# The self-attention block's feed-forward products, each taken from three products of rounded parts and rests

## The reference, cut to what matters

```python
y = y @ Wo + x
z = _rms_norm(y, ln2_w)
z = jax.nn.relu(z @ W1) @ W2      # W1 256x1024, W2 1024x256
return z + y
```

## Time and profile before

| | |
|---|---|
| median of 3 runs | 1431.43 us (1429.8 to 1434.38) |
| the profiled execution | 1430.63 us, of which 1428.8 us are its span |
| mean granted TensorE clock | 0.961 of full |
| PE busy | 1275.9 us, 89% |
| PE weight loads | 929.8 us, 65% |
| DVE busy | 766.8 us, 54% |
| ACT busy | 583.0 us, 41% |
| POOL busy | 390.7 us, 27% |

### The profile page before, as it was taken

One profiled execution on the slowest core, in us unless ns is written; L12 is line 12 of the kernel. 1 busy time (PEld: TensorE's weight loads), 2 busy tenths in 40 slices (PEclk: granted clock), 3 DMA queues, 4 the chain that ended last, 5 costly groups with the idle time before them and its releaser, 6 DMA issues.

```text
span 1428.8 us, 27261 instructions
## 1 busy us (share of the span) xinstructions
PE 1275.9 (89%) x8838; PEld 929.8 (65%) x8839; DVE 766.8 (54%) x2053; ACT 583.0 (41%) x1253; POOL 390.7 (27%) x680
## 2 busy tenths in 40 slices
PE   6588999999999999999999999999987449999997
PEld 4365776767777776767777777767765325555554
DVE  5645566676766666676666666676643241121111
ACT  3424436363545536363544536363522212222221
POOL 2311121212141221213141221213122124444443
PEclk9598999999999999999999999999999669999999
DMA  8300000000000000000000000000054002112111
GB/s 273 97 8 9 16 1 31 1 29 0 29 29 0 29 0 29 0 29 0 29 29 0 29 0 29 0 29 22 2 192 177 30 22 62 53 56 60 59 55 38
DMA packets 44135, 56.69 MB, mean 40 GB/s; under 512 B 6486, under 2 KB 38016, under 8 KB 44097
## 3 DMA queue, kind: packets, MB, share of 16 engines
q1 hardware_dynamic: 37824, 41.23, 8.8%
q0 software_dynamic: 5616, 14.43, 3.5%
q10 hardware_dynamic: 656, 0.52, 0.1%
HBM read 40.44 MB, written 16.65 MB: 40 GB/s over the span
## 4 chain that ended last, share of the span: by engine, by line
PE 75%; DVE 10%; ACT 8%; issue 5%; POOL 1%; DMA 0%; ACTq 0%; DVEq 0%; SPq 0%; POOLq 0%
PE bank L1337 69%; PE bank L1372 2%; ACT a_p L725 2%; ACT shared L730 2%; PE bank L1519 2%; DVE a_p L1140 2%; DVE shared L1114 1%; PE bank L1664 1%; DVE a_sq L1108 1%; ACT shared L759 1%; ACT b_qh L659 1%; DVE a_split L1084 0%; DVE a_split L1083 0%; DVE shared L1291 0%; DVE a_split L1082 0%
## 5 line engine op out<-in xcount | busy, mean ns | idle before, releaser
L1337 PE MATMUL bank<-shared 128*128 128x256 f32 (+4 forms) x2242 | 447.8, 380 | 44.9 <-ACT shared L670 13.8
L1337 PEld LDWEIGHTS bank<-shared 128*128 128x128 f32 (+2 forms) x2242 | 318.1, 173 | 125.5 <-issue 31.5
L1140 DVE TENSOR_TENSOR a_p<-a_p,eb 128x385 f32<-128x385 f32 x256 | 126.2, 556 | 89.5 <-ACT a_p L725 89.5
L1337 PE MATMUL bank<-up,shared 128*128 x312 | 144.5, 606 | 11.0 <-issue 11.0
L725 ACT ACTIVATE a_p<-bank 128x385 f32<-128x385 f32 x256 | 105.1, 503 | 42.0 <-PE bank L1337 41.9
L869 POOL TENSOR_SCALAR a_rz<-a_ms 128x2 f32<-128x2 f32 x16 | 3.1, 191 | 431.7 <-ACT a_sq L736 431.7
L1337 PE MATMUL bank<-a_xnT,w 128*128 128x256 f32 x512 | 114.7, 382 | 1.4 <-ACT a_xnT L622 1.4
L1337 PE MATMUL bank<-w,a_hT 128*128 128x256 f32 x512 | 113.1, 379 | 0.0
L1314 DVE TENSOR_TENSOR shared<-bank,shared 128x512 f32<-128x512 f32 x39 | 27.0, 692 | 154.4 <-ACT shared L757 84.7
L622 ACT COPY a_xnT<-bank 128x512 f32<-128x512 f32 x32 | 18.8, 587 | 220.2 <-PE bank L1372 220.2
L1337 PEld LDWEIGHTS bank<-a_xnT,w 128*128 128x128 f32 x512 | 96.0, 190 | 18.1 <-issue 3.4
(11 more groups left out here) (206 smaller groups left out, 2037.9 us busy)
## 6 DMA issues: line engine op xcount, KB each, us to landing
up<-in_L_ffn_up_w SPq DMA_DIRECT2D x8, 1024.0 KB, 14.4
x_in<-in_x SPq DMA_DIRECT2D x16, 256.0 KB, 2.7
shared<-in_ctx SPq DMA_DIRECT2D x16, 256.0 KB, 3.0
rows_x<-shared SPq DMA_DIRECT2D x16, 256.0 KB, 2.9
rows_skip<-shared SPq DMA_DIRECT2D x16, 256.0 KB, 3.1
down<-in_L_ffn_down_w SPq DMA_DIRECT2D x8, 512.0 KB, 12.5
toep<-a_hT SPq DMA_DIRECT2D x1, 3072.0 KB, 10.2
eb<-toep SPq DMA_DIRECT2D x4, 512.0 KB, 6.2
```

Source lines behind the costliest of these rows:

```text
L1140: tt(a_p[:, n_ % NPA], a_p[:, n_ % NPA], eb[:, n_], ALU.mult).then_inc(sig["a_p"], 1)
L1337: return mm(out, lhsT=lhsT, rhs=rhs, start=first, stop=last, **kw)
```

## The change

Each of the two weights is split into a rounded part (float32r) and the rest, and so are the activations. A float32 product becomes three float32r products: rounded by rounded, rest of the weight by rounded activation, rounded weight by rest of the activation. This holds from turn 3 on (`SPLIT_FROM`), in 14 turns; turns 1 and 2 work as before.

- In turn 2, ahead of `PLAN`, ACT writes the rounded W1 and W2 aside (two copies of 128x2048) and DVE subtracts (two of 128x2048); SP stores the two rests in DRAM, 1 MB each. In turn 3, ahead of `PLAN`, ACT rounds both weights in place, in four copies of 128x1024.
- In each turn from 3 on SP loads the two rests, 1 MB each, into room that the turn no longer needs: W1's over `a_qT` and `a_kT` once the last score of A is done, W2's over `a_p` once the last weighing of A is done.
- ACT's copy of `A.z` and its four ReLUs now write rounded parts. DVE makes the rests from PSUM with one instruction of 128x512 each: one for `A.z`, four for `A.h`, put between its other work. The bank is free only after DVE's instruction.
- `A.h0` to `A.h3` get four banks (1, 2, 3, 0) instead of two.
- Buffers are laid out anew so that float32r names lie over the float32 ones.

The diff, cut to its core:

```diff
-    add((2, 3), [f"A.h{n}" for n in range(4)])
+    add((1, 2, 3, 0), [f"A.h{n}" for n in range(4)])
...
+SPLIT = ("w01", "w02",)
+SPLIT_FROM = 3
...
@@ SP, in turn
+            if it.first == SPLIT_FROM - 1:
+                for n, name in enumerate(SPLIT):
+                    sp.wait_ge(s_low, n + 1)
+                    sp.dma_start(low_of[name].ap(), made_low[n % 2].bitcast(F32)).then_inc(s_low_out[name], 16)
+                for name in SPLIT:
+                    sp.wait_ge(s_low_out[name], 16)
             if "C" in it.stages:
...
+            if "A" in it.stages and it.first >= SPLIT_FROM:
+                full(sp, it, f"A.s{H0 - 1}")
+                sp.dma_start(flat(w01_low[:]).bitcast(F32), low_of["w01"].ap()).then_inc(s_low_in["w01"], 16)
+                after(sp, "a_p_used", it.batch("A"))
+                sp.dma_start(flat(w02_low[:]).bitcast(F32), low_of["w02"].ap()).then_inc(s_low_in["w02"], 16)
@@ ACT
+        def round_aside(which):
+            for n in which:
+                if n == 0:
+                    act.wait_ge(s_w, 4 * C + 3)
+                if n == 2:
+                    act.wait_ge(s_low_out[SPLIT[0]], 16)
+                copy(made_low[n % 2], flat(weight[SPLIT[n]][:])).then_inc(s_hi, 1)
+        def round_in_place(names):
+            act.wait_ge(s_low, len(SPLIT))
+            for name in names:
+                for half in range(2):
+                    part = slice(half * HID, (half + 1) * HID)
+                    copy(flat(weight_hi[name][:])[:, part], flat(weight[name][:])[:, part]).then_inc(s_round, 1)
...
+            if it.first == SPLIT_FROM - 1:
+                round_aside((0, 1))
+            if it.first == SPLIT_FROM:
+                round_in_place(SPLIT)
             for what, st, n in PLAN:
...
+            if A and it.first >= SPLIT_FROM:
+                copy(flat(a_zT_hi[:]), full(act, it, "A.z")[:]).then_inc(sig["a_zhi"], 1)
...
+                    if it.first >= SPLIT_FROM:
+                        nc.scalar.activation(flat(a_hT_hi[:, 2 * n:2 * n + 2]), ps[:], ACT.Relu).then_inc(sig["a_hhi"], 1)
@@ DVE
+        def low_parts(which):
+            for n in which:
+                dve.wait_ge(s_hi, n + 1)
+                tt(made_low[n % 2], flat(weight[SPLIT[n]][:]), made_low[n % 2].bitcast(F32), ALU.subtract).then_inc(s_low, 1)
+        def rest(it, job, dst, hi, name, n=None):
+            ps = full(dve, it, job)
...
+            if n:
+                ins = dve.scalar_tensor_tensor(flat(dst), ps[:], 0.0, flat(hi).bitcast(F32), ALU.max, ALU.subtract)
+            else:
+                ins = tt(flat(dst), ps[:], flat(hi).bitcast(F32), ALU.subtract)
+            ins.then_inc(e_sem(job), 1)
...
+            if it.first == SPLIT_FROM - 1:
+                low_parts((0, 1))
             for what, st, n in PLAN:
...
+            if A and it.first >= SPLIT_FROM:
+                rest(it, "A.z", a_zT_low[:], a_zT_hi[:], "a_zhi")
+            if Bb:
                 stats(b_q, b_st, b_mv2, "b_stats2", "b_mv2", b)
...
                 stats(x_in, a_st, a_mv, "a_stats", "a_mv", p)
+            if A and it.first >= SPLIT_FROM:
+                rest_of_hidden(it, (0, 1))
...
                 shifted(b_q, b_q, b_mv2, b_rs2[:, 1], "b_q")
+            if A and it.first >= SPLIT_FROM:
+                rest_of_hidden(it, (2,))
...
                 taken(dve, it, "D.out")
+            if A and it.first >= SPLIT_FROM:
+                rest_of_hidden(it, (3,))
+            if Dd:
                 stats(b_f, c_st, c_mv, "c_stats", "c_mv", dd)
@@ PE
+        def split_cols_out(it, job, xT, xT_low, w, w_low, first_chunk, hi_ready=None):
+            ps = claim(pe, it, job)
+            for m in range(2):
+                at = slice((first_chunk + m) * P, (first_chunk + m + 1) * P)
+                for c in range(C):
+                    product(ps[:, m * S:(m + 1) * S], w[:, c, at], xT[:, c, :], c == 0, False)
+                for c in range(C):
+                    product(ps[:, m * S:(m + 1) * S], w_low[:, c, at], xT[:, c, :], False, False)
+                if m == 0 and hi_ready:
+                    taken(pe, it, hi_ready)
+                for c in range(C):
+                    ins = product(ps[:, m * S:(m + 1) * S], w[:, c, at], xT_low[:, c, :], False,
+                                  c == C - 1)
+            ins.then_inc(f_sem(job), 1)
...
                 for n in range(4):
+                    if it.first >= SPLIT_FROM:
+                        split_cols_out(it, f"A.h{n}", a_zT_hi, a_zT_low, w01_hi, w01_low, 2 * n, "A.z" if n == 0 else None)
...
+                            product(out, a_hT_hi[:, j, tok(t)], w02_hi[:, j, :], j == 0, False)
+                            product(out, a_hT_hi[:, j, tok(t)], w02_low[:, j, :], False, False)
+                            ins = product(out, a_hT_low[:, j, tok(t)], w02_hi[:, j, :], False, j == J - 1)
```

More of the change, by code:

```diff
@@ L45 @@
 TILES_MAX = NT + E - 1
-SHARED = 22980
+SHARED = 23040
 QUARTERS = 4
@@ L351, in _build, with doubles @@
[L351 to L354, removed]
+    def doubles(stack, sizes, wanted):
+        made, at = {}, 0
+        for name, words in sizes:
+            if name not in wanted:
+                sbuf(stack, f"under_{name}", [P, words])
+                continue
+            alias, shape = wanted[name]
+            made[alias] = sbuf(stack, alias, shape, F32R)
+            if words > C * HID and name != "made0":
+                sbuf(stack, f"above_{name}", [P, words - int(np.prod(shape[1:]))])
+        return made
@@ new lines, in _build @@
+    starts = sorted((place[name], name) for name in place)
+    sizes = [(name, nxt - at) for (at, name), (nxt, _) in zip(starts, starts[1:] + [(SHARED, None)])]
+    at_f = [name for name, _ in sizes].index("b_f")
+    sizes[at_f:at_f + 3] = [("made0", C * HID)]
+    whole_shared.close()
+    r1 = doubles(ctx, sizes, {
+        "w11": ("w11_hi", [P, C, HID]), "b_zT": ("d_qT_hi", [P, C, S]), "b_yT": ("d_qT_low", [P, C, S]),
+        "b_p": ("w11_low", [P, C, HID]), "b_hT": ("a_hT_low", [P, J, S]), "made0": ("made0", [P, C, HID])})
@@ L981, in subtract_maxima, with rest_of_hidden @@
                 tt(eb[:, heads, 0:S], eb[:, heads, 0:S], top, ALU.subtract).then_inc(s_eb, 1)
+        def low_parts(which):
[4 more added lines that the diff above has]
+            ps = full(dve, it, job)
+            first = SPLIT_FROM - 1 if name[0] == "a" else 0
+            wait(dve, sig[name], (it.batch("D" if name == "d_qhi" else "A") - first) * PER_BATCH[name] + (n or 1))
+            if n:
+                ins = dve.scalar_tensor_tensor(flat(dst), ps[:], 0.0, flat(hi).bitcast(F32), ALU.max, ALU.subtract)
+            else:
+                ins = tt(flat(dst), ps[:], flat(hi).bitcast(F32), ALU.subtract)
+            ins.then_inc(e_sem(job), 1)
+        def rest_of_hidden(it, which):
+            for n in which:
+                part = slice(2 * n, 2 * n + 2)
+                rest(it, f"A.h{n}", a_hT_low[:, part], a_hT_hi[:, part], "a_hhi", n + 1)
         def stats(x, st, mv, s_stats, s_mv, batch):
@@ L1592, in turn @@
             if A:
-                taken(pe, it, "A.z")
+                if it.first == SPLIT_FROM:
+                    pe.wait_ge(s_round, 2 * len(SPLIT))
+                if it.first >= SPLIT_FROM:
+                    wait(pe, sig["a_zhi"], a - (SPLIT_FROM - 1) + 1)
+                    wait(pe, s_low_in["w01"], (a - (SPLIT_FROM - 1)) * 16 + 16)
+                else:
+                    taken(pe, it, "A.z")
                 if it.first == 1:
```

118 lines of the change are left out of this document (81 added, 37 removed).

## The result

| | before | after |
|---|---|---|
| median | 1431.71 us (1429.8 to 1434.38) | 1451.16 us (1450.08 to 1452.61) |
| profiled span | 1428.8 us | 1448.4 us |
| PE busy | 1275.9 us | 1254.6 us |
| DVE busy | 766.8 us | 816.0 us |

The ratio is 1.0135, 95% interval 1.0116 to 1.0154: slower by 19.5 us, where 12.5 us were forecast (1444, range 1431 to 1465). PE is busy for 21 us less, and the kernel is 20 us longer.

What follows compares the result with a forecast made beforehand. PE looked like the bound, with a second chain only 0.43 us behind at B.q_, so PE's saving turns into waits. Once-only work 11.2 plus boundaries 1.3 made +12.5 us: 1444 us predicted, range 1431 to 1465.

Steps and rivals of the forecast that it cites:

- the first part: Opening on what bounds the kernel: PE has no wait at a turn's end, but another chain reaches B.q_ almost as late.
- the second chain: POOL's c_norm, DVE's stage C work, c_norms, b_xl's factor, b_xl, L1031, ACT's b_xT, up to B.q_; runs beside PE.
- the 0.43 of the text: Slack at B.q_, 0.43 us a turn: a turn can shrink by only that, 6 us over all turns.
- the 64.0 to 64.6 that the text named as a sign: Steady turn length in us, listed under what would show the forecast; under 63.6 us would show it wrong.
- the forecast's own ends: Limits given per term: once-only work 7 and 15 us, thirteen turn boundaries -2 and +6.5 us.
- PE's part: A.h and A.out: 96 products at 0.115 us (0.108 to 0.120) instead of 13.91 us, 2.7 us less a turn.
- The rival of a slot twice as long: Float32r product costs over 0.125 us; with 0.217, PE needs 20.8 us, +6.9 in 14 turns, 1540 us; chance 0.09.
- The steady turn: Turns 3 to 15: c_norm 0.53 us later against 0.43 slack, +0.10 a turn (-0.14 to +0.5), +1.3 us over 13 boundaries.
- The once-only work: Turns 2 and 3, ahead of the scores: +5.0, +4.0 and +2.2 for low clock, sum 11.2 us, ends 7 and 15.
- DMA at nothing: SP's two 1 MB loads a turn land before W1's and W2's rests are wanted, hidden behind PE's work: cost nothing.
- Turn 16 at nothing, at most -2,: Turn 16 leads into a turn without stage A: nothing taken for it, at most a gain of 2 us.
- The clock in every turn: Rival: PE's 3.3 us of waits in 12 lower its clock each turn, about 2 us lost a turn, 1470 us; chance 0.11.

Runs made afterwards that it cites:

- e4: Changed kernel without DVE's five rests a turn, products reading the rounded activations instead (result wrong): 1436.8 us, steady turn 63.93 us.
- e6: Changed kernel with POOL, DVE and ACT reordered so the second chain no longer waits on stage C's work: 1406.16 us, steady turn 61.93 us.
- e8: Changed kernel with DVE's rest of A.h3 moved behind the statistics of b_f, all work kept: 1440.82 us, steady turn 64.09 us.
- e2: Changed kernel with only the once-only work moved, behind PLAN on ACT and later on DVE: 1440.89 us, steady turn 64.88 us.
- e3: Changed kernel without the two 1 MB loads a turn, products reading the rounded weights again (result wrong): 1450.22 us, steady turn 64.90 us.
- e5: Kernel before the change with the same reordering of POOL, DVE and ACT as e6: 1423.09 us, steady turn 64.12 us.
- e10: e9 with the reordering of e6 (64 products, result lacks the activations' rests): 1395.65 us, turns 60.59 and 62.30 us.
- e11: e10 with x1 and its statistics ahead of stage C's two products on DVE: 1353.77 us, steady turn 58.17 us.
- e9: e4 with 64 float32r products a turn instead of 96 (result lacks the activations' rests): 1446.59 us, steady turn 64.85 us.

## Why the prediction was right, and what was off

- **The mechanism held.** PE's gain turned into waits at `B.q_` (1.44) and the places ahead of it, as the first part said: the second chain has next to no slack. e4 bounds the gain at 0.20 us a turn against the 0.43 of the text, and e6, in which that chain is pulled forward, gets all of the 2.2 us.
- **The size was less good than the range makes it look.** 12.5 us were forecast and 19.5 came, and the steady turn of 64.90 us lies outside the 64.0 to 64.6 that the text named as a sign. The time stayed within what the forecast's own ends add up to (1431.4 + 15 + 6.5 = 1453) because the room that was kept for the once-only work was not needed.
- **PE's part.** 0.118 for a product, inside 0.108 to 0.120; 13.05 against 15.26 us is 2.2 less instead of 2.7. The rival of a slot twice as long is out. By the Trainium skill ("TensorE: Matmul & The Clock Gate", Part 3, "What overlaps and what doesn't") weight loads overlap with matmuls in flight only when the row group differs. Here each product has its own load with all rows, each load's record lasts 0.19 us, and a product starts every 0.118. This rule and the rows don't agree, and the rows decide.
- **The steady turn is the term that was mis-sized**: +0.10 forecast (ends -0.14 and +0.5), +0.77 measured, outside its ends. It was forecast as the delay of the second chain, 0.53, less 0.43 of slack. Measured were a delay of 0.98, a slack of 0.35, and 0.14 more that was lost behind `B.q_`'s start. Of the 0.45 more delay, 0.14 is the slot (the text's own steps give about 0.67 for 0.118, between 0.53 and 0.76). Another 0.17 is DVE's, whose statistics ended 1.78 later and not 1.46. And 0.12 is the first instruction of `c_norm`, which took 0.34 instead of 0.22; the trace doesn't show why (POOL's L918 took 0.22 behind a longer wait, at 674.76). Each is small; they add up because a chain without slack passes every one on. The slack is smaller than the text had it because `B.q_` starts 0.14 behind `b_xT`'s end and not 0.06. That the delay comes from DVE's rests ahead of the statistics of `b_f` is shown by e4 (-0.97 without them) and e8 (-0.81 with one moved). Where the 0.14 at the end is lost was not tried.
- **The once-only work**: 10.5 against 11.2. Turn 2 came out at +5.0, in part by luck. PE's first weighing (118.86) comes only 4.3 later, counted from `A.z`, since the copies took 1.91 and the subtractions 2.29 (1.98 and 2.40 forecast) and ACT began them 0.3 earlier. The other 0.7 came behind it, where the granted clock was 0.50 from 120 to 125 us and had been 1.00; the text had taken nothing for that. Turn 3 was +5.5, not 6.2: PE's first record behind the copies (185.46) comes 3.8 later, and what follows, begun at 0.52, cost 1.7 and not 2.2. e2 shows that all of it hangs on the place.
- **DMA at nothing** held (e3).
- **Turn 16 at nothing, at most -2,** was wrong: what follows the last `A.z` grew by 1.2. In turn 17 `B.x` waits 4.48 us where it waited 1.77, so PE's saving is gone again, and `B.q_` starts 0.7 later, counted from `A.z`. e5 shows that this place was worth 6.8 us already before the change, from waits that the earlier trace rows had shown and the text had read only for the clock.
- **The clock in every turn** (rival, 0.11) didn't come true: the granted clock is 1.00 in all steady turns of after, with waits of 0.73, 0.17 and 1.44 close together. In e10, with one wait of 2.3 us a turn, it falls in each second turn, and in e11, without that wait, it stays at 1.00. The Trainium skill (the same page, "A second HAM failure mode: psum-queue depth-cycling") tells of a kernel in which frequent short idles between groups of matmuls made the clock swing; after's trace doesn't show that, e10's comes near it.
- **A wait that the text didn't name**: `A.qk` on `x1` (0.73), through the bank of `A.out`. It was covered in after, as PE would have waited at `B.q_` anyway, but it is what held e9 and e10 back.

## What to carry to other kernels

An engine that is busy all the time can have a second chain right behind it: before a change makes it faster, measure how much earlier each of its inputs could be there, and take the edit only together with a reorder that pulls those inputs forward. Ask of each instruction in that chain whether its place in its engine's order is there for its data or by habit; a bank is held for as long as its reader's queue is held. Put once-only work where the path has slack, which can be a few lines further down.

## What the runs showed of the hardware that was not expected

- Work taken away can lengthen a turn: e9 has 3.7 us less on PE than e4 and is 0.9 us longer, since behind one idle stretch of 3.6 us the granted clock was 0.54, close to the lower of its two levels (1.2 of 2.4 GHz), for the next 6.5 us. With the wait gone (e11) the same work runs at 1.00.
- Equal waits needn't cost the same: in e10 2.29 us left the clock at 1.00, 2.31 a turn later brought it to 0.68 to 0.76, in alternation from turn to turn (60.59 and 62.30).
- Small POOL instructions that depend on each other follow each other more closely in the straight-line code of turn 3 than in the loop: 0.08 us lie between the end of one and the start of the next (209.45 + 0.19 to 209.72) against 0.18 in the loop (the last line). This is perhaps why turn 4, which begins behind turn 3's chain, was 0.46 us shorter than in before; that was only read from the trace, not tried.

```profile
209.45 0.19 POOL L973 TENSOR_SCALAR a_rz<-a_ms 128x2 f32<-128x2 f32 x1 [32.29 <-ACT a_sq L837]
209.72 0.70 POOL L912 TENSOR_TENSOR a_rz<-a_rz,mhalf 128x2 f32<-128x2 f32 x1
```

```profile
662.93 0.70 POOL L912 TENSOR_TENSOR a_rz<-a_rz,mhalf 128x2 f32<-128x2 f32 x1 [0.18 <-POOL a_rz L973]
```
